# One chunk in 128 of the attention layers fetched by ScalarE, and the linear part of elu made by VectorE

## What is computed

```python
src, dst = add_self_loops(edge_index, n)
h = relu(gcn_conv(layernorm(x), src, dst, W_gcn, b_gcn))
h = batch_norm(h, g0, beta0)
h = gat_conv(h, src, dst, W1, a_src1, a_dst1, b1)        # attention layer 1
h = elu(batch_norm(h, g1, beta1))
h = gat_conv(h, src, dst, W2, a_src2, a_dst2, b2)        # attention layer 2
x = x + elu(batch_norm(h, g2, beta2))
x = x + ffn(layernorm(x))                                # 8 experts, 2 per node

def gat_conv(x, src, dst, W, a_src, a_dst, b):
    h = (x @ W).reshape(n, 4, 64)
    e = leaky_relu((h * a_src).sum(-1)[src] + (h * a_dst).sum(-1)[dst], 0.2)
    w = exp(e - segment_max(e, dst)[dst])
    out = segment_sum((w / segment_sum(w, dst)[dst])[:, :, None] * h[src], dst)
    return out + b
```

## Time and profile before

| | |
|---|---|
| time, median of 3 runs | 8129.97 us (8129.04 to 8130.97) |
| the profiled execution | 8128.7 us, span 8126.9 us |
| edge stage, first layer: POOL's first to last gather | 356 to 2370 us, then the input of attention layer 1 |
| edge stage, attention layer 1: POOL's first to last gather | 2476.03 to 4543.73 us |
| input of attention layer 2: first exponent to last window | 4631.1 to 4732.9 us |
| edge stage, attention layer 2: POOL's first to last gather | 4754.21 to 6818.65 us |
| feed-forward layer | from 6832 us |
| busy in the span | PE 58%, DVE 58%, ACT 21%, POOL 62% |

### The profile page before, as it was taken

One profiled execution on the slowest core, in us unless ns is written; L12 is line 12 of the kernel. 1 busy time (PEld: TensorE's weight loads), 2 busy tenths in 40 slices (PEclk: granted clock), 3 DMA queues, 4 the chain that ended last, 5 costly groups with the idle time before them and its releaser, 6 DMA issues. The chain is left out here.

```text
span 8126.9 us, 152076 instructions
## 1 busy us (share of the span) xinstructions
PE 4740.2 (58%) x25092; PEld 3771.0 (46%) x25110; DVE 4678.9 (58%) x11632; ACT 1678.8 (21%) x7056; POOL 5035.3 (62%) x5320
## 2 busy tenths in 40 slices
PE   3444444444454666666656756565665556779994
PEld 3433333333343444444444544444444444559993
DVE  7722222222237777777777767777677777764445
ACT  3400000000022111111111431111111112563331
POOL 0177777777755777777777247777777774015552
PEclk9999999999997777877777787778787876869997
DMA  5411111111124555555555245555555553412226
GB/s 203 162 29 29 29 29 29 29 29 29 29 56 132 137 137 137 137 137 138 136 134 139 69 121 138 137 137 137 137 137 138 137 137 85 140 51 70 70 70 219
DMA packets 527200, 848.14 MB, mean 104 GB/s; under 512 B 147632, under 2 KB 373137, under 8 KB 519791
## 3 DMA queue, kind: packets, MB, share of 16 engines
q0 software_dynamic: 228576, 543.07, 26.7%
q1 hardware_dynamic: 265512, 274.99, 11.7%
q10 hardware_dynamic: 32358, 23.60, 0.9%
HBM read 750.78 MB, written 82.11 MB: 102 GB/s over the span
## 5 line engine op out<-in xcount | busy, mean ns | idle before, releaser
L769 POOL DMA_INDIRECT gat_rows<-gat_table,gat_idx x3278 | 3103.4, 947 | 1057.8 <-issue 944.7
L890 PE MATMUL gat_ps_sum<-gat_msg,gat_hot 128*128 128x260 f32 x6656 | 2267.8, 500 | 1263.5 <-DVE feat L909 1261.0
L890 PEld LDWEIGHTS gat_ps_sum<-gat_msg,gat_hot 128*128 128x128 f32 x6656 | 1562.4, 246 | 1605.0 <-DVE gat_msg L945 1150.5
L769 POOL DMA_INDIRECT gcn_rows<-gcn_table,gcn_idx x1614 | 1523.0, 944 | 787.4 <-issue 478.3
L890 PE MATMUL gcn_ps_sum<-gcn_rows,gcn_hot 128*128 128x64 f32 x3328 | 814.1, 426 | 1228.2 <-DMA gcn_rows<-gcn_table,gcn_idx 724.7
L890 PEld LDWEIGHTS gcn_ps_sum<-gcn_rows,gcn_hot 128*128 128x128 f32 x3328 | 741.1, 328 | 1301.2 <-DMA gcn_rows<-gcn_table,gcn_idx 658.3
L909 DVE SCALAR_TENSOR_TENSOR feat<-gcn_ps_sum,in_first,feat 128x64 f32 x416 | 118.0, 284 | 1572.2 <-PE gcn_ps_sum L890 1572.2
L873 PEld LDWEIGHTS gat_ps_near<-gat_tab,gat_hot_t 128*128 128x128 bf16 x6656 | 268.3, 101 | 766.4 <-issue 579.2
L945 DVE TENSOR_TENSOR gat_msg<-gat_rows,gat_ps_as 128x1024 f32<-128x1024 f32 x416 | 503.2, 1210 | 118.1 <-issue 117.4
L921 DVE TENSOR_TENSOR gat_hot<-gat_count,mod_t 128x512 f32<-128x512 f32 x832 | 566.4, 681 | 2.7
L873 PE MATMUL gat_ps_near<-gat_tab,gat_hot_t 128*128 128x24 bf16 x6656 | 309.8, 178 | 435.4 <-DVE gat_hot L921 431.3
(11 more groups left out here) (308 smaller groups left out, 6375.5 us busy)
## 6 DMA issues: line engine op xcount, KB each, us to landing
gat_mod<-mod_rows SPq DMA_DIRECT2D x832, 128.0 KB
gat_ahead<-gat_table SPq DMA_DIRECT2D x6400, 1.0 KB
gi_mods<-mod_rows SPq DMA_DIRECT2D x52, 1024.0 KB, 4.7
gat_rows<-gat_table,gat_idx POOLq DMA_INDIRECT x3278
gcn_ahead<-gcn_table SPq DMA_DIRECT2D x3200, 0.2 KB
gcn_ahead<-gcn_table ACTq DMA_DIRECT2D x3200, 0.2 KB
gcn_rows<-gcn_table,gcn_idx POOLq DMA_INDIRECT x1614, 2.4
gat_table<-feat SPq DMA_DIRECT2D x28, 910.0 KB, 5.3
```

Source lines behind the costliest of these rows:

```text
L769: pool.indirect_dma_start(B["rows"][:, j, k, :], None, table, bass.IndirectOffsetOnAxis(ap=B["idx"][:, j, k:k + 1], axis=0)).then_inc(rows ...
L890: mm = pe.matmul(B["ps_sum"][b][:, 0:width], B["hot"][:, j, k, :], rhs, start=(k == 0), stop=(k == CH - 1))
```

## The change

One constant table replaces `AHEAD` and `ATS`: (16, 2), (16, 9) in the first layer, which is what was there, and (16, 2), (32, 9) in the attention layers. So in an attention layer ACT fetches the last chunk of the groups 41, 73, ..., 393 (12 groups), 128 rows each, four in a turn, and pushes them four turns ahead of the group; POOL leaves these 12 chunks out. The common body of POOL, PE and DVE grows from 16 to 32 turns there, ACT's from 16 to 64. `pace` takes a new number `spare`, with which the loops of SP and ACT stop earlier: SP's loop now covers turns 64 to 351 of an attention layer (`last` is (416 - 16 - 18) // 32 = 11, where it was 12), with jumps back up to turn 320; what follows is straight code. In the input of attention layer 2 `straight` is gone from ACT, and DVE's `line` makes that part into the same buffer, one quadruple ahead.

```diff
-AHEAD = 16
-ATS = (2, 9)
-BURST = P // AHEAD
+HELPERS = {False: ((16, 2), (16, 9)), True: ((16, 2), (32, 9))}
...
-    last = (n - max(leads)) // ring
+    last = (n - max(leads) - spare) // ring
...
-            for k in range(CH - len(ahead(i, c))):
+            for k in range(CH - len(ahead(TURN, i, c))):
...
-        pace(pool, NG, [(group, 0)], AHEAD)
+        pace(pool, NG, [(group, 0)], TURN)
...
-            if c % AHEAD == at - 1 and known(n):
+            if c % period == at - lead and known(n):
...
-        pace(sp, NG, ([(mods, 0)] if gat else []) + [(bring, AHEAD), (fetch, 0), (push, -AHEAD)], 2 * AHEAD)
+        pace(sp, NG, ([(mods, 0)] if gat else []) + [(bring, period), (fetch, 0), (push, -period)], 2 * period,
+             period + helpers[0][1])
...
-        if gat:
-            pace(act, NG, [(weigh, 2), (stage, RING + 2)], AHEAD)
-        else:
-            bring, fetch, push = helper(act, 1)
-            pace(act, NG, [(push, -AHEAD), (stage, RING), (bring, AHEAD), (fetch, 0)], 2 * AHEAD)
+        bring, fetch, push = helper(act, 1, 4 if gat else 1)
+        steps = [(weigh, 2), (stage, RING + 2)] if gat else [(stage, RING)]
+        pace(act, NG, [(push, -period)] + steps + [(bring, period), (fetch, 0)], turn,
+             period + helpers[1][1])
...
                 def line(q):
-                    if q >= SLOTS:
+                    to = shf if elu else stage
+                    if elu:
+                        wait(dve, staged, q - (SLOTS - 1))
+                    elif q >= SLOTS:
                         dve.wait_ge(product, last(q - SLOTS))
...
-                turns(NQ, [(clip, 0), (unite, 0)] if elu else [(line, 0)])
+                turns(NQ, [(clip, 0), (line, 1), (unite, 0)] if elu else [(line, 0)])
...
-                turns(NQ, ([(expo, 2), (straight, 2)] if elu else []) + [(place, 0)])
+                turns(NQ, ([(expo, 2)] if elu else []) + [(place, 0)])
```

More of the change, by code:

```diff
@@ L60, in __call__, with pace @@
         self.eng.wait_ge(self.sem, self.start + self.n)
-def pace(eng, n, steps, ring=2):
+def pace(eng, n, steps, ring=2, spare=0):
     leads = [lead for _, lead in steps]
@@ L741, in fast_edges, with landed, ahead @@
     rows_used = msg_made if gat else summed
[L742 to L760, removed]
+    helpers = HELPERS[gat]
+    TURN = max(period for period, _ in helpers)
+    pushed = [M.sem(f"{L}pushed{h}") for h in range(len(helpers))]
+    ahead_free = [M.sem(f"{L}ahead_free{h}") for h in range(len(helpers))]
+    idx_in = [[M.sem(f"{L}ahead_idx_in{h}{b}") for b in range(2)] for h in range(len(helpers))]
+    ahead_in = [[M.sem(f"{L}ahead_in{h}{b}") for b in range(2)] for h in range(len(helpers))]
+    def landed(turn, i, c):
+        each, rest = CH * turn // RING, CH * (c // RING + 1)
+        for period, at in helpers:
+            if c % RING == at % RING and not (isinstance(i, int) and turn * i + c < period + at):
+                each, rest = each - turn // period, rest - (c - at) // period
+        return 16 * each * i + 16 * rest
+    def ahead(turn, i, c):
+        return [(h, 16 * (turn // period) * i + 16 * ((c - at) // period)) for h, (period, at) in enumerate(helpers)
+                if c % period == at and not (isinstance(i, int) and turn * i + c < period)]
     def gather(pool):
         def group(i, c):
-            j, g = c % RING, AHEAD * i + c
+            j, g = c % RING, TURN * i + c
             pool.wait_ge(idx_staged, g + 1)
@@ L771, in group, with helper @@
                                         ).then_inc(rows_in[j], 16)
-        pace(pool, NG, [(group, 0)], AHEAD)
[L774 to L778, removed]
+        pace(pool, NG, [(group, 0)], TURN)
+    def helper(eng, h, lead=1):
+        period, at = helpers[h]
+        own, burst = at % RING, P // period
+        regs = [eng.alloc_register(f"{L}row{h}_{r}") for r in range(burst)]
+        count = (NG - 1 - at) // period
         def known(n):
@@ L825, in mods @@
                          ).then_inc(mod_in[j], 16)
-        pace(sp, NG, ([(mods, 0)] if gat else []) + [(bring, AHEAD), (fetch, 0), (push, -AHEAD)], 2 * AHEAD)
+        period = helpers[0][0]
+        pace(sp, NG, ([(mods, 0)] if gat else []) + [(bring, period), (fetch, 0), (push, -period)], 2 * period,
+             period + helpers[0][1])
     def act_program(act):
         regs = [act.alloc_register(f"{L}act_w{j}") for j in range(RING)]
-        per = 1 if gat else 2
+        period = helpers[1][0]
+        turn = 2 * period
         def stage(i, c):
-            j, g = c % RING, per * AHEAD * i + c
+            j, g = c % RING, turn * i + c
             used = c - RING
-            wait(act, rows_in[j], landed(per * i, used))
-            for h in ahead(per * i, used):
-                wait(act, pushed[h], 16 * (per * i + used // AHEAD))
+            wait(act, rows_in[j], landed(turn, i, used))
+            for h, count in ahead(turn, i, used):
+                wait(act, pushed[h], count)
             act.copy(B["idx"][:, j, :], at1(K["src_t"], g)).then_inc(idx_staged, 1)
@@ L883, in total @@
                 pe.wait_ge(hot_built, g + 1)
-                pe.wait_ge(rows_in[j], landed(i, c))
-                for h in ahead(i, c):
-                    pe.wait_ge(pushed[h], 16 * (i + c // AHEAD))
+                pe.wait_ge(rows_in[j], landed(TURN, i, c))
+                for h, count in ahead(TURN, i, c):
+                    pe.wait_ge(pushed[h], count)
             wait(pe, added, g - 1)
@@ L892, in total @@
             mm.then_inc(summed, 1)
-        pace(pe, NG, [(total, 1), (look, 3)] if gat else [(total, 0)], AHEAD)
+        pace(pe, NG, [(total, 1), (look, 3)] if gat else [(total, 0)], TURN)
     def dve_program(dve):
@@ L947, in dve_program @@
         steps = [(messages, 1), (add, -1), (logits, 2), (hots, 3)] if gat else [(add, 0), (hots, 3)]
-        pace(dve, NG, steps, AHEAD)
+        pace(dve, NG, steps, TURN)
     return dict(gather=gather, send=send, act=act_program, pe=pe_program, dve=dve_program)
@@ L1507, in expo @@
                     ins.then_inc(exped, 1)
-                def straight(q):
-                    wait(act, staged, q - (SLOTS - 1))
-                    for k in range(KP):
-                        ins = act.activation(some(shf, q, k), feat[:, four(q), k * P:(k + 1) * P], ACT.Identity,
-                                             scale=scale[:, k:k + 1], bias=shift[:, k:k + 1])
-                    ins.then_inc(shifted, 1)
                 def place(q):
```

50 lines of the change are left out of this document (25 added, 25 removed).

## The result

The changed kernel takes 8107.7 us (median of 10 runs, 8105.0 to 8113.0) against 8129.7 us of the kernel before in the same session (10 runs, 8127.2 to 8134.4): 0.9973 of it, with a 95% interval from 0.9963 to 0.9983. That is 22.0 us less where 21.9 were forecast. The profiled execution of the changed kernel has a span of 8109.0 us. The total hides terms that missed in opposite directions.

What follows compares the result with a forecast made beforehand. SP's queue was taken to bound the attention edge stages, not POOL; gains of 7.7 (layer 1), 7.0 (layer 2) and 7.2 us (input) sum to 21.9, from 8128.7 to 8106.8, plus 1.3 for the median: 8108 us, range 8091 to 8120.

Steps and rivals of the forecast that it cites:

- SP's queue sets the lasting pace: Attention edge stages: SP needs 159.9 and 159.7 us for 32 groups, 2.3 more than POOL, so SP limits.
- The last jump back is at turn 320, and what lies behind it is gained: Edge stages from the gather held at SP's last jump: 6.4 us gained in layer 1, 6.05 in layer 2.
- SP's pace stays, since the steps in its turn are the same: SP's queue in the attention loops: time for 32 groups unchanged, mods still 159.8 us apart.
- The input: Input of attention layer 2: without `straight` on ACT, PE limits at 0.89 us a window; 7.2 us gained.
- One sign: Input of attention layer 2: no wait of DVE for ACT should be seen there after the change.
- ACT's new work at nothing: Attention layers: ACT's four rows a turn, 1.6 us, fit its free time; cost 0, bounds 0 to 1 us a layer.
- the slower rival: ACT's rows lengthen SP's turn: 0.046 us a turn uses up the gain, 0.15 gives 8179 us; chance 0.06.
- the prediction's own price of 476 turns: SP runs free from turn 82 to 320 in both layers, so any growth of its turn is paid 476 times.
- POOL's pauses: Attention layers: POOL pauses some 3.6 us once per 32 groups from about turn 192, the last ahead of group 325.
- POOL decides: Rival for the edge stages: SP is not the pace, all 24 gathers count, 30.0 us; 8093 us; chance 0.13.
- The jump stays: Rival: SP leaving its loop at turn 352 costs as much as jumping back; 14.7 us gained, 8115; chance 0.09.
- Transfers set the pace: Rival: DMA transfers, not their issue, limit; attention layers gain nothing, 7.2 us remain, 8123; chance 0.03.

Runs made afterwards that it cites:

- sp_four_incs: Changed kernel with four more semaphore increments in each of SP's attention-layer turns and no added transfer; x is their time a turn, 0.27 us; 8286.9 us.
- mods_on_act: Changed kernel with the mods transfer of each turn moved from SP's queue to ACT's; 8084.8 us, 0.9943 of the kernel before.
- sp_loop_long: Changed kernel with SP's loop as long as before, so SP jumps back once more, at turn 352, and its code keeps its old places; 8116.4 us.
- only_helper: Changed kernel without its input part: ACT fetches its chunks, but `straight` is back on ACT; 8118.7 us.
- sp_pad: Changed kernel with 50 semaphore increments ahead of SP's first turn in each attention layer, shifting its loop's code; 8100.2 us.
- only_input: Kernel before with the input part alone: `line` on DVE instead of `straight` on ACT; 8119.9 us.
- sp_pad_198: Changed kernel with 198 semaphore increments behind SP's last turn in the first layer's and layer 1's edge stages, shifting later SP code; 8105.2 us.

## Why the prediction was right, and where it was not

**SP's queue sets the lasting pace: right.** sp_four_incs and mods_on_act show it from both sides, each within 2 us of what was expected (for sp_four_incs with the x that its trace gave).

**The last jump back is at turn 320, and what lies behind it is gained: right, forecast a little large.** From the first gather of group 325 to the last one, layer 1 takes 4532.24 - 4087.31 = 444.9 us; before it took 450.5. That is 5.6 where 6.4 were forecast. The difference is in part a new pause of 0.71 us ahead of group 341. In layer 2 it is 4.7 (446.0 against 450.7) where 6.05 were forecast; there the pause ahead of group 357 did not go, it is still 1.53 us. sp_loop_long brings the jump back, and with it a pause of 3.48 us in layer 1.

**"SP's pace stays, since the steps in its turn are the same": wrong.** This is the step that failed. The steps are the same, but the jump and the stops of SP are part of the pace, and they changed with the place of SP's code: layer 1 lost one stop of 0.35 us a loop and 0.6 us of the jump, layer 2 took on the longer jump. SP's 32 groups went from 159.8 to 159.35 us in layer 1 and from 159.4 to 160.0 in layer 2. Over the loops ahead of turn 320 this adds up: group 325 comes 6.3 us earlier in layer 1 (4087.31 - 2476.43 = 1610.9 against 1617.2), where 1.25 were forecast, and in layer 2 3.4 us later (6351.21 - 4734.04 = 1617.2 against 1613.8 in the trace of before) where it should have come 0.95 earlier. The misses, 5.1 us too little and 4.4 too much, nearly cancel. So the attention layers gave 13.2 us by the profiles, 12.0 by the median of only_helper, where 14.7 were forecast, and that the total came right is luck: it was an accident of where the code lay, and the input gave more than forecast. sp_pad, with both layers at cheap places, takes 8100.2 us.

**The input: right.** Windows come 0.89 us apart throughout, 83.66 us for 94. `line` takes 1.00 us for both passes, between the bounds and next to the 2 x 0.54 of the row chosen. The 8.7 us between the layers in this execution are 1.5 more than the 7.2 forecast, and the other kernels show 6 to 7.5. By the medians only_input gives 10.7, more than the 7.2. One sign was put wrongly: DVE still waits for ACT, 0.82 us in each quadruple, for `expo`; it costs nothing since PE is the limit.

**ACT's new work at nothing: too low; against the slower rival: right.** Eight rows on SP's queue take 3.19 us while ACT issues its four. But summed over turns 128 to 320, SP's row issues and the loads of their source numbers take 82.7 to 83.0 us per 32 turns in ten loops with ACT's rows beside them (changed, only_helper, sp_loop_long, sp_pad, sp_pad_198), and 82.5 to 82.6 in the four without (before, only_input). That is 0.35 us, 0.011 us a turn. The slower rival needed 0.046 to use the gain up, but by the prediction's own price of 476 turns it is some 5 us that stood at nothing. That SP's 32 groups are, over both layers, 159.7 us against 159.6 before hides it, since the price of the jumps changed too. sp_loop_long, with SP's code at its old places, shows it: 160.25 and 159.7 us for 32 groups, against 159.8 and 159.4 in before and 159.8 and 159.3 in only_input.

**POOL's pauses.** They come once in 32 groups, as said, but later: from group 261 in layer 1 and 229 in layer 2, not from about 192, and the long ones last 2.7 to 3.6 us.

**The rivals.** "POOL decides" is what mods_on_act makes true, not the change alone. "The jump stays" was put at 8115; with the jump, sp_loop_long takes 8116.4, but the two agree by luck: the fetch gave 3.5 us beside only_input where the rival had 7.5, and the input 10.7 where it had 7.2. "Transfers set the pace" falls with sp_four_incs.

## What to carry to other kernels

Taking work from the busiest engine is worth no more than the distance to the next pace: here 12 us of 30, most of them with SP's shorter loop, until the next one, SP's queue, was relieved of a transfer that another queue had time for. So compare the turn times of all queues, DMA issue and the loop's jump back included, before choosing what to move. And a loop whose jump back lies on the path makes every edit of that engine's code, even far away, a change of several microseconds, so a gain of that size needs the gaps at the jumps looked at before a cause is named.

## What the runs showed of the hardware that was not expected

- The same loop body on SP's queue shows a gap of about 3.0 or about 4.0 us at its jump back, depending on the place of its code, and stays with that value in every turn of the loop (2.8 to 3.6 against 3.7 to 4.6). The dear value comes where a stop falls one or two records ahead of the branch. Where both have eight stops, the loop as a whole differs by less, 0.4 to 0.6 us in 32 turns: where layer 2 jumps cheaply in sp_loop_long and sp_pad_198, the stop lies in the rows ahead of the jump, which take 3.55 and 3.54 us instead of 3.2.
- SP stands still for 0.35 us after every 128 of its records, in loops and in straight code.
- A semaphore increment costs SP 0.07 us (0.27 for four), a sixth of what the issue of a row costs it (3.19 / 8 = 0.40 us).
- Two queues that issue single rows at the same time hardly slow each other: 0.40 us a row on both. Beside ACT's four rows a turn, SP's rows with their loads take 0.4% longer (82.9 against 82.5 us per 32 turns).
